# Two 512-column turns and sixteen block copies per second batch: another place in VectorE's order, and all copies on VectorE

## What is computed

```python
w = weights[conditions]                      # layer 0: one 128 x 128 matrix per batch
x = x + einsum('bct,bcd->bdt', x, w)
q, k, v = x @ Wq.T, x @ Wk.T, x @ Wv.T       # layer 1: 16 heads of 64
q = q * min(cond, 4)
attn = softmax(where(causal, q @ k.T / 8, min))
x = x + (attn @ v) @ Wo.T
```

## Time and profile before

| | us |
|---|---|
| median of 3 runs | 1581.62 (1580.28 to 1583.79) |
| profiled execution, its own time | 1581.07 |
| its span, first to last instruction | 1579.6 |
| TensorE busy | 1551.8 (98%) |
| VectorE busy | 1040.6 (66%) |
| ScalarE busy | 854.8 (54%) |
| GpSimd busy | 854.3 (54%) |

### The profile page before, as it was taken

How to read it: one execution, slowest core, us unless ns; L and a number is a source line. 1 busy time by engine, 2 the same in 40 slices (tenths; PEclk the granted TensorE clock), 3 DMA queues, 4 the chain that set the end, 5 groups by cost and what they waited for, 6 DMA issues and landing times.

```text
span 1579.6 us, 23477 instructions
## 1 busy us (share of the span) xinstructions
PE 1551.8 (98%) x7459; PEld 1299.9 (82%) x7459; DVE 1040.6 (66%) x1865; ACT 854.8 (54%) x2312; POOL 854.3 (54%) x752
## 2 busy tenths in 40 slices
PE   9999999999999999999999999999999999999999
PEld 7777777777888888888888888888888878888887
DVE  5866667665377777777776677777777645555553
ACT  6656566564266666666656666666666622222220
POOL 2545545454255665567555566675576644555552
PEclk9999999999999999999999999999999999999999
DMA  9957888865866776776767566667666696444442
GB/s 327 332 193 268 301 268 308 274 217 224 313 181 199 212 208 179 216 209 180 201 195 249 174 161 206 202 170 210 182 192 169 218 354 248 166 166 160 167 160 87
DMA packets 192300, 341.46 MB, mean 216 GB/s; under 512 B 23986, under 2 KB 116402, under 8 KB 185010
## 3 DMA queue, kind: packets, MB, share of 16 engines
q1 hardware_dynamic: 191026, 331.59, 65.6%
q10 hardware_dynamic: 1152, 8.39, 1.4%
HBM read 184.70 MB, written 134.22 MB: 202 GB/s over the span
## 4 chain that ended last, share of the span: by engine, by line
PE 89%; DVE 8%; issue 1%; DMA 1%; SPq 1%; POOL 1%; ACT 1%; DVEq 0%; POOLq 0%
PE p_PJ L768 20%; PE p_PJ L769 20%; PE p_PJ L770 20%; PE p_SC L768 5%; PE p_SC L769 5%; PE p_SC L770 5%; PE p_PV L873 4%; DVE t_XR L1260 3%; PE p_LP L768 1%; PE p_PV L770 1%; PE p_PV L768 1%; PE p_PV L769 1%; PE p_LP L770 1%; PE p_LP L769 1%; DVE t_TT L1254 1%
## 5 line engine op out<-in xcount | busy, mean ns | idle before, releaser
L768 PE MATMUL p_PJ<-t_XH,t_WH 128*128 128x512 f32 x1008 | 394.2, 391 | 0.0
L769 PE MATMUL p_PJ<-t_XL,t_WH 128*128 128x512 f32 x1008 | 394.2, 391 | 0.0
L770 PE MATMUL p_PJ<-t_XH,t_WL 128*128 128x512 f32 x1008 | 392.2, 389 | 0.0
L1118 ACT ACTIVATE t_PP<-t_PP,t_st 128x128 f32<-128x128 f32 x512 | 199.5, 391 | 175.5 <-DVE t_st L1314 173.9
L1438 POOL TENSOR_TENSOR t_PP<-t_PP,t_st 128x512 f32<-128x512 f32 x128 | 133.2, 1041 | 205.1 <-DVE t_st L1318 205.1
L770 PEld LDWEIGHTS p_PJ<-t_XH,t_WL 128*128 128x128 f32 x1008 | 189.3, 188 | 40.4
L768 PEld LDWEIGHTS p_PJ<-t_XH,t_WH 128*128 128x128 f32 x1008 | 190.0, 189 | 33.7
L769 PEld LDWEIGHTS p_PJ<-t_XL,t_WH 128*128 128x128 f32 x1008 | 190.0, 189 | 32.3
L1332 DVE TENSOR_REDUCE t_AT<-p_PV 64x256 f32<-64x512 f32 x252 | 171.2, 679 | 24.3 <-ACT t_AC L1136 12.3
L1444 POOL TENSOR_TENSOR t_AT<-t_AT,t_AC 128x256 f32<-128x256 f32 x126 | 117.1, 929 | 125.6 <-DVE t_AT L1332 125.6
L1441 POOL TENSOR_TENSOR t_PS<-t_PT,t_PS 128x512 fp32r<-128x512 f32 x122 | 157.7, 1293 | 0.0
(11 more groups left out here) (259 smaller groups left out, 3607.1 us busy)
## 6 DMA issues: line engine op xcount, KB each, us to landing
t_XH<-xth_scratch SPq DMA_DIRECT2D x56, 512.0 KB, 6.5
t_XL<-xtl_scratch SPq DMA_DIRECT2D x56, 512.0 KB, 6.8
t_PT<-t_TB SPq DMA_DIRECT2D x580, 32.0 KB, 2.3
v_scratch<-t_VR SPq DMA_DIRECT2D x64, 256.0 KB, 4.2
xth_scratch<-t_XH SPq DMA_DIRECT2D x16, 1024.0 KB, 4.0
xtl_scratch<-t_XL SPq DMA_DIRECT2D x16, 1024.0 KB, 6.7
t_VX<-v_scratch SPq DMA_DIRECT2D x32, 512.0 KB, 5.7
at_scratch<-t_AT SPq DMA_DIRECT2D x126, 128.0 KB, 3.4
```

Source lines behind the costliest of these rows:

```text
L768: pe.matmul(bank, lh, rh, start=first, stop=False, skip_group_check=goes_on)
L769: pe.matmul(bank, lh, rl, start=False, stop=False, skip_group_check=goes_on)
L770: return pe.matmul(bank, ll, rh, start=False, stop=last, skip_group_check=goes_on)
L1118: act.activation(PP[:, u, h, :], PP[:, u, h, :], ACT.Exp, bias=st[:, 0, u, h:h + 1], scale=1.0, accum_out=st[:, 1, u, h:h + 1]).then_inc(a ...
```

## The change

For the even batches from 6 on, the two turns and the two sets of copies are issued later, and so are the high and low parts made from them. The times in the diff are counted from p, which for an even batch is tick -2 of the frame in which it is turned. So the turns move from ticks 2.25 and 5.5 of the frame to 8.5 and 13, the copies from 3.5 and 6.5 to 9.25 and 13.75, x_high from 8 and 8.75 to 17.25 and 18, and x_low from 9 and 9.75 to 18.25 and 19. `ACT_MOVES` becomes empty: VectorE makes eight copies per half where it made four.

```diff
@@ plan_l0_pair
                 if turned_by_dve(bb):
-                    l0_turn.put(p + (4.25, 7.5)[h], (bb, h))
-                    l0_move.put(p + (5.5, 8.5)[h], (bb, h))
-                    x_high.put(p + 10 + 0.75 * h, (bb, h))
-                    x_low.put(p + 11 + 0.75 * h, (bb, h))
+                    l0_turn.put(p + (10.5, 15)[h], (bb, h))
+                    l0_move.put(p + (11.25, 15.75)[h], (bb, h))
+                    x_high.put(p + 19.25 + 0.75 * h, (bb, h))
+                    x_low.put(p + 20.25 + 0.75 * h, (bb, h))
@@
-        ACT_MOVES = ((0, 2, 5, 7), (0, 2, 5, 7))
+        ACT_MOVES = ((), ())
```

## The result

| | us | ratio to before |
|---|---|---|
| before | 1581.62 (1580.28 to 1583.79) | |
| changed kernel | 1590.62 (1590.20 to 1591.75) | 1.0058 [1.0043, 1.0072] |

The change costs 9.0 us; 6.3 were forecast, as 1587.9 us. The profiled execution took 1590.62, its span is 1589.3, 9.7 above that of before, at a mean granted clock of 0.994 instead of 0.998. The other four executions of the changed kernel have 0.992 to 0.994, and the kernel before has 0.998 or 0.999 in each of the twenty executions beside the experiments.

The account below looks back on a forecast made before the run. TensorE, 98% busy, was taken as the bound, its waits while VectorE turns batches costing 19.7 us. Added waits 17.1 + 6.8 + 2.1 = 26.0, less 19.7, give +6.3 on 1581.62: 1587.9 us, range 1577 to 1595.

Parts of the forecast that it names:

- The wait at product 3: TensorE waits for the first gather, behind VectorE's turns; with the gather ahead of them, 19.7 us come back.
- The walk through the frame: VectorE's list timed from product 0: second copies from 12.18, second gather 17.58, product 5 at 18.41 instead of 16.27.
- Copies let through one per GpSimd operation: Second eight copies on VectorE: a copy meeting a GpSimd operation waits it out; GpSimd first waits 0.2 us for copy 3.
- +4.1: Net us for the whole change if GpSimd ran from the moment it asks, with waits of 1.96 and 1.48 at product 5.
- rival D: Second eight copies: GpSimd doesn't get in between them, no wait at product 5, 19.7 us come back, 1561.9 us; chance 0.18.
- A new wait in 13 frames: TensorE waits at product 5 for the second gather: 2.14 us in eight frames, 1.69 in four, 2.1 in frame 0; 26.0 us.
- the 3.2 us set in the prediction: Whole kernel: 0.2% of the time, the least difference that a measurement can tell from no change.
- B: First eight copies meet GpSimd's first group too: 6.5 us more over 13 frames, 1594.4 us; chance 0.06.
- C: A draw: waits at product 5 average between 1.3 and 1.75 us, time within 3.2 us of before; chance 0.16.
- The third gather and x_low: On VectorE after the second gather: line 1265 ends near 18.8, third gather near 20, before product 6 at 21.6.

Follow-up runs that it names:

- e3: Changed kernel, but GpSimd's first xl of an even batch waits until VectorE's second eight copies are done: 1560.80 us, ratio 0.9868.
- e5: Changed kernel, but the first of a frame's two Wq or Wk pieces is split at tick 16.5, not 10.5, behind the second gather: 1580.91 us, ratio 0.9996.
- e2: Kernel before, turns at their old places, but all copies on VectorE and none on ScalarE: 1641.37 us, ratio 1.0377.
- e1: Changed kernel with the turns at the new places, but ScalarE keeps its four copies of each eight: 1561.78 us, ratio 0.9874.

## Why the prediction was right, and where it was short

*The wait at product 3 goes*: right. Forecast 19.7 us, measured 19.7.

*The walk through the frame*: right nearly step by step. Counted from product 0 at 197.85, forecast against measured: first turn 6.93 and 6.93, first copies 7.68 and 7.66, third sum's low half 10.21 and 10.18, second turn 11.43 and 11.39, second copies 12.18 and 12.13, GpSimd's ask 12.88 and 12.84, end of the copies 16.97 and 16.79, gather 17.58 and 17.40, product 5 18.41 and 18.22. Product 5 was due at 16.11, where 16.27 was forecast, so that the wait of 2.11 us is as forecast because the gather and the due time were both early by nearly the same. All of it came from rows of the kernel before, and from the order in which the lists are walked.

*Copies let through one per GpSimd operation, GpSimd waiting out the copy under way*: right, but waiting cost GpSimd less than was charged. The xl starts at 210.69 with 0.21 us of a free copy left and takes 1.36 us instead of 1.29: it loses 0.07 us, where the walk had 0.2. Over the frames of the changed kernel an xl with 0.21 us of a copy left takes 1.36, one with 0.19 left 1.34, and one with 0.13 or less left 1.29, so by an estimate from these rows GpSimd needs the copy to be done only 0.14 us after its own recorded start. (The +4.1 that the prediction gives for a GpSimd that runs at once adds up to 4.0.) That GpSimd gets in between copies 0.03 us apart was the point on which rival D hung; it does. D's price was right too: e3 brings about what D describes, 1560.8 us against its 1561.9.

*A new wait in 13 frames, 26.0 us*: too many. Frame 12 has none, since there is no further even batch after the one turned in it, so there is no xl to meet. The trace of the changed kernel shows it: no GpSimd operation until 395.58, eight copies in 2.51 us and the gather at 390.89 in time.

```profile
387.73 2.51 DVE L1260 COPY t_XR<-t_TT 32x256 f32<-32x256 f32 x8
390.28 0.69 DVE L1269 TENSOR_TENSOR t_SL<-t_SUM,t_SH 128x512 fp32r<-128x512 f32 x1
390.89 0.68 DVE L1218 TENSOR_TENSOR t_GA<-p_PJ,t_GA 128x512 f32<-128x512 f32 x1
```

The other twelve came to 24.0 us, where the forecast had 24.3 for them. With the 19.7 removed the waits net +4.3 us where +6.3 was forecast, and with the small steps of -1.9 us, which the sum did not have, +2.4. That alone would have been a draw by the 3.2 us set in the prediction, as e5 is.

*The term that was missing*: the granted clock, +7.9 us. The sum priced a wait at its length. In these runs no wait of 1.5 to 1.7 us was followed by half clock (the kernel before, e5, three frames of the changed kernel), nor any of up to 2.0. Of the changed kernel's eight waits of 2.1 to 2.2 us five were, and all of those of 4 us in e2. So the mechanism was right, and that the total came within 2.7 us of the forecast is in part luck: 7.9 us of clock were missing, against 2.0 too many of waits, 1.9 of small steps and 0.8 near 1295 us.

*Rivals.* B, the first eight copies caught as well: no, 2.49 us for them from frame 1 on; in frame 0 alone 2.83, as foreseen there. C, a draw, would have come about without the clock. The third gather and x_low stayed off the path, as forecast, but for 0.15 us in each of two frames.

*What stays open.* Why some waits of 2.1 us are followed by half clock and others are not, in the changed kernel mostly every second one. Taken from start to start over all traces, none of 39 waits of 1.1 to 2.0 us was followed by half clock, 16 of 25 waits of 2.0 to 2.6 us were, and all thirteen of 3.7 to 5.6 us in e2 had it behind them or already during them. So longer waits are needed in these kernels, and place and engine are not decisive; the exact condition stays open. That the copies and GpSimd exclude each other is shown by when they run (e3 against the changed kernel); that it is a port which they share is not shown.

## What to carry to other kernels

Before a piece of work is moved between engines, ask what the engine that gives it up will start earlier. Here ScalarE's copies were holding back a GpSimd operation by 1.8 us (in e1 it starts 200.23 - 197.71 = 2.52 behind the first copy, in the changed kernel 210.69 - 209.98 = 0.71), and without them it ran into the very copies that had been moved. Move the late work first, by itself (e1: -20 us), and then try each further edit alone. And when a wait of TensorE grows from about 1.5 to above 2 us, look at the granted clock by frame before believing that it costs only its length.

## What the runs showed of the hardware

A wait of TensorE of 2.1 us, in a stretch in which it is otherwise never idle, can be followed, 0.6 to 1.4 us after its end, by a stretch at 1.2 GHz that costs 1.6 us: three quarters of the wait again. It was in five of eight cases in the changed kernel. Eleven waits of 1.63 to 1.65 us (e5) cost nothing beyond their length.

GpSimd's operation, arriving amid copies that VectorE issues 0.03 us apart, waits at most for the one under way and then runs; the next copy waits. So the mean VectorE copy is 0.41 us in the changed kernel and 0.29 in e3, and neither engine starves the other. By the order rule of the Trainium skill, page "SBUF — State Buffer", section "Who interferes with whom", the one that issues second waits until the other's instruction is done; the trace agrees, with 1.27 us for a copy behind the xl and 1.36 instead of 1.29 for the xl behind a copy, though the xl loses only 0.07 of the 0.21 us that the copy had left.
